# Four layer norms computed with a Newton root on VectorE instead of ScalarE's tables

## The reference, cut to what matters

```python
def _layernorm(x, axis=-1, eps=1e-05):
    m = jnp.mean(x, axis=axis, keepdims=True)
    v = jnp.var(x, axis=axis, keepdims=True)
    return (x - m) / jnp.sqrt(v + eps)
...
x = x + 0.5 * _L0_ffn_ref(_layernorm(x, axis=-1), ...)
x = x + _L0_attn_ref(_layernorm(x, axis=-1), ...)
x = x + 0.5 * _L0_ffn_ref(_layernorm(x, axis=-1), ...)
x = x + 0.5 * _L1_ffn_ref(_layernorm(x, axis=-1), ...)
x = x + _L1_attn_ref(_layernorm(x, axis=-1), ...)
x = x + 0.5 * _L1_ffn_ref(_layernorm(x, axis=-1), ...)
```

## Time and profile before

| | us |
|---|---|
| median of 3 runs | 1140.63 |
| lowest and highest | 1140.47, 1144.98 |
| the profiled execution, its own time | 1144.14 |
| span of its trace | 1142.4 |
| TensorE matmuls busy | 954.2 (84%) |
| VectorE busy | 672.9 (59%) |
| ScalarE busy | 626.3 (55%) |
| GpSimd busy | 349.1 (31%) |
| mean granted clock of TensorE | 0.894 of full |

### The profile page before, as it was taken

How to read it: one execution, slowest core, us unless ns; L and a number is a source line. 1 busy time by engine, 2 the same in 40 slices (tenths; PEclk the granted TensorE clock), 3 DMA queues, 4 the chain that set the end, 5 groups by cost and what they waited for, 6 DMA issues and landing times.

```text
span 1142.4 us, 12658 instructions
## 1 busy us (share of the span) xinstructions
PE 954.2 (84%) x4387; PEld 637.8 (56%) x4395; DVE 672.9 (59%) x1247; ACT 626.3 (55%) x986; POOL 349.1 (31%) x257
## 2 busy tenths in 40 slices
PE   6899997599999998689999974998567777675998
PEld 4678884233333333257888852886344554443797
DVE  2888885567777877437888826242645545226222
ACT  5455554378888887645555554445342544443443
POOL 1597775000000000006777725201011121204300
PEclk8999998789999999969999987999768877775999
DMA  5225110000000000033122101100000000001001
GB/s 162 40 83 155 58 66 8 0 1 1 1 1 0 1 1 1 0 97 73 64 64 65 47 1 55 38 1 1 1 2 3 3 3 2 2 1 37 1 1 37
DMA packets 30932, 33.61 MB, mean 29 GB/s; under 512 B 2254, under 2 KB 19990, under 8 KB 30870
## 3 DMA queue, kind: packets, MB, share of 16 engines
q1 hardware_dynamic: 30870, 32.82, 10.0%
HBM read 31.36 MB, written 1.18 MB: 28 GB/s over the span
## 4 chain that ended last, share of the span: by engine, by line
PE 63%; DVE 20%; ACT 10%; POOL 3%; issue 3%; DMA 0%; SPq 0%; ACTq 0%; DVEq 0%; POOLq 0%
PE ps L122 10%; PE ps L123 9%; PE ps L124 9%; PE ps L595 5%; PE ps L732 5%; DVE smax L1697 3%; PE ps L753 2%; PE ps L589 2%; PE ps L814 2%; PE ps L487 2%; PE ps L573 2%; ACT L1139 2%; ACT ex L1258 2%; PE ps L493 2%; PE ps L704 2%
## 5 line engine op out<-in xcount | busy, mean ns | idle before, releaser
L1800 POOL TENSOR_TENSOR fl<-fp,fh 128x512 fp32r<-128x512 f32 x144 | 225.6, 1588 | 128.5 <-ACT fh L1062 128.4
L1053 ACT ACTIVATE fs<-ps 128x512 f32<-128x512 f32 x144 | 86.2, 599 | 115.6 <-PE ps L124 115.3
L1396 DVE TENSOR_TENSOR fp<-fp,cwb 128x512 f32<-128x512 f32 x128 | 139.0, 1086 | 13.7 <-DVE fp L1389 0.5
L1389 DVE TENSOR_TENSOR fp<-fs,ps 128x512 f32<-128x512 f32 x144 | 98.1, 682 | 38.8 <-ACT fs L1053 37.6
L122 PE MATMUL ps<-z_hi,w_hi 128*128 128x512 f32 x288 | 116.7, 405 | 3.4 <-DVE fp L1389 3.3
L123 PE MATMUL ps<-z_lo,w_hi 128*128 128x512 f32 x288 | 115.7, 402 | 0.0
L124 PE MATMUL ps<-z_hi,w_lo 128*128 128x512 f32 x288 | 114.1, 396 | 0.0
L1062 ACT CAST fh<-fp 128x512 fp32r<-128x512 f32 x144 | 88.8, 617 | 34.7 <-DVE fp L1396 30.2
L1865 POOL TENSOR_TENSOR ln_sq<-ln_rs 128x512 f32<-128x512 f32 x20 | 21.1, 1056 | 272.8 <-ACT ln_rs L1102 272.8
L1858 POOL TENSOR_SCALAR_AFFINE_SELECT ex<-ex 128x1024 f32<-128x1024 f32 (+1 forms) x24 | 33.7, 1403 | 171.8 <-ACT ex L1258 171.8
L1697 DVE TENSOR_REDUCE smax<-ps 128x8 f32<-128x2048 f32 (+1 forms) x24 | 55.0, 2291 | 34.0 <-PE ps L828 27.3
(11 more groups left out here) (245 smaller groups left out, 2021.7 us busy)
## 6 DMA issues: line engine op xcount, KB each, us to landing
cwb<-cw_spread SPq DMA_DIRECT2D x64, 256.0 KB, 3.2
w_raw<-in_L_ffn_w_dram SPq DMA_DIRECT2D x20, 256.0 KB, 3.1
w_raw<-in_L_ffn_w_dram SPq DMA_DIRECT2D x4, 512.0 KB, 6.2
w<-in_L_ffn_w_dram SPq DMA_DIRECT2D x8, 256.0 KB, 5.4
x_tok<-in_L_attn_x_dram SPq DMA_DIRECT2D x4, 256.0 KB, 3.9
wb<-in_L_attn_W_dram SPq DMA_DIRECT2D x1, 1024.0 KB, 7.1
wb<-in_L_attn_W_dram SPq DMA_DIRECT2D x4, 256.0 KB, 4.1
stk<-mT SPq DMA_DIRECT2D x64, 4.0 KB
```

What stands on the lines that cost most here:

```text
L1053: act.activation(fs[:, n % 2, :], ps[:, n % 2, :], ACT.Silu).then_inc(silu_done, 1)
L1389: dve.tensor_tensor(f, fs[:, n % 2, :], ps[:, 2 + n % 2, :], ALU.mult).then_inc(prod_done, 1)
L1396: dve.tensor_tensor(f, f, cwb[:, x % CW_RING, :], ALU.mult).then_inc(weighed, 1)
L1800: pool.tensor_tensor(fl[:, n % RING0, :], fp[:, n % RING0, :], f32(fh[:, n % RING0, :]), ALU.subtract).then_inc(flo_done, 1)
```

## The change

The norms A to D take another path, and the table loads and the logarithms and exponentials of these four go. For a block `tb` of norm `n`:
- `ln_centre` on TensorE as before, but into banks of `LN_BANK`.
- `ln_square` on ScalarE, and `ln_copy`, which moves the centred block to `z`.
- `ln_variance` on TensorE: four matmuls with 128 tokens' squares as weights and one column of `mean_w`, so that the variance lies with tokens on partitions, one column for each 128 tokens.
- `ln_root` on VectorE: eleven small instructions, each of which waits for the one before, for blocks 0 to 2 together (12 columns) and then for block 3 (4 columns). A bit trick gives the first guess and three Newton steps follow.
- `ln_spread` on TensorE: four matmuls with one column of the root, repeated 128 times, as weights and the identity as the moving side, which lays the root out over the partitions again.
- `ln_scale` on VectorE multiplies; where halves are wanted, `ln_high` and `ln_low` follow.

The centring, squares and copies of blocks 0 to 2 are put into the end of the stage before, block 3 comes behind. The scores of `ffn1` go to bank 4 and move ahead of `ffn1` into the code of the norm.

```diff
-        XT1, SC1, PT1, GI1 = (4, 5, 6, 7), 0, 1, 2
...
+        XT1, SC1, PT1, GI1 = (5, 6, 7, 0), 4, 1, 2
...
+        LN_BANK = {LN_FFN0B: (4, 5, 6, 7), LN_FFN1: OUT0, LN_ATTN1: (0, 1, 6, 7), LN_FFN1B: (0, 1, 3, 5)}
+        LN_VAR = {LN_FFN0B: 3, LN_FFN1: 0, LN_ATTN1: 4, LN_FFN1B: 6}
...
+            def ln_centre(n, tb):
+                pe.wait_ge(ln_in, NTB * n + tb + 1)
+                pe.matmul(ps[:, LN_BANK[n][tb], :], centre[:], blk(xr, tb), start=True, stop=True).then_inc(lxc_ready, 1)
...
+            def ln_variance(n, tb):
+                pe.wait_ge(lsq_ready, later(n, tb))
+                for q in range(TPB):
+                    c = tb * TPB + q
+                    ins = pe.matmul(ps[:, LN_VAR[n], c:c + 1], LN_SQ[n][:, tb, q * P:(q + 1) * P], mean_w[:, 0:1], start=True, stop=True)
+                ins.then_inc(lvar_ready, 1)
+            def ln_spread(n, tb):
+                pe.wait_ge(root_ready, later(n, tb))
+                pe.wait_ge(lxc_copied, later(n, tb))
+                for q in range(TPB):
+                    ins = pe.matmul(ps[:, LN_BANK[n][tb], q * P:(q + 1) * P], ln_r[:, tb, q:q + 1].broadcast_to([P, P]), ident[:],
+                                    start=True, stop=True)
+                ins.then_inc(spread_ready, 1)
...
+            def scores(n, tb):
+                pe.wait_ge(z_ready, NTB * n + tb + 1)
...
-                logits(0)
-                up(0)
+                if call == 1:
+                    for tb in range(NTB - 1):
+                        ln_spread(ln, tb)
+                    ln_variance(ln, NTB - 1)
+                    pe.wait_ge(z_ready, u0 + 1)
+                    up(0)
+                    ln_spread(ln, NTB - 1)
+                    logits(0)
...
                 for n in range(ALL0 - LAG0, ALL0):
                     down(n)
+                    if call == 1 and n < ALL0 - 1:
+                        ln_centre(LN_FFN1, n - ALL0 + LAG0)
+                if call == 1:
+                    for tb in range(NTB - 1):
+                        ln_variance(LN_FFN1, tb)
+                    ln_centre(LN_FFN1, NTB - 1)
+                    for tb in range(NTB - 1):
+                        ln_spread(LN_FFN1, tb)
+                    ln_variance(LN_FFN1, NTB - 1)
+                    for tb in range(NTB - 1):
+                        scores(LN_FFN1, tb)
+                    ln_spread(LN_FFN1, NTB - 1)
+                    scores(LN_FFN1, NTB - 1)
...
+                for tb in range(NTB - 1):
+                    ln_centre(LN_FFN0B, tb)
+                for tb in range(NTB - 1):
+                    ln_variance(LN_FFN0B, tb)
...
+                ln_centre(LN_FFN0B, NTB - 1)
...
+                    if call == 0 and n == SEQS - 1:
+                        ln_centre(LN_ATTN1, 0)
+                        ln_centre(LN_ATTN1, 1)
...
+                if call == 0:
+                    ln_centre(LN_ATTN1, 2)
                 scatter(SEQS - 1)
...
-                layer_norm(u0, lambda tb: blk(xr, tb))
...
+                for tb in range(NTB - 1):
+                    ln_variance(LN_ATTN1, tb)
+                ln_centre(LN_ATTN1, NTB - 1)
+                for tb in range(NTB - 1):
+                    ln_spread(LN_ATTN1, tb)
+                ln_variance(LN_ATTN1, NTB - 1)
+                pe.wait_ge(y_done, NTB * HALVED.index(LN_ATTN1) + 2)
                 pe.wait_ge(z_ready, u0 + 1)
                 project_in(0, 0)
+                ln_spread(LN_ATTN1, NTB - 1)
                 pe.wait_ge(z_ready, u0 + NTB)
                 project_in(0, 1)
+                pe.wait_ge(cmask_done, 1)
...
+                    if s == SEQS:
+                        for t in range(NTB - 1):
+                            ln_centre(LN_FFN1B, t)
...
                 turn(NTB - 1)
+                for tb in range(NTB - 1):
+                    ln_variance(LN_FFN1B, tb)
                 project_out(NTB - 1)
+                for tb in range(NTB - 1):
+                    ln_spread(LN_FFN1B, tb)
+                ln_centre(LN_FFN1B, NTB - 1)
+                ln_variance(LN_FFN1B, NTB - 1)
+                for tb in range(NTB - 1):
+                    scores(LN_FFN1B, tb)
+                ln_spread(LN_FFN1B, NTB - 1)
+                scores(LN_FFN1B, NTB - 1)
...
+            def ln_square(n, tb):
+                act.wait_ge(lxc_ready, later(n, tb))
+                act.activation(LN_SQ[n][:, tb, :], ps[:, LN_BANK[n][tb], :], ACT.Square).then_inc(lsq_ready, 1)
+            def ln_copy(n, tb):
+                act.wait_ge(lxc_ready, later(n, tb))
+                act.copy(blk(z, tb), ps[:, LN_BANK[n][tb], :]).then_inc(lxc_copied, 1)
...
+                ln_square(LN_ATTN1, 3)
+                ln_copy(LN_ATTN1, 3)
+                ln_high(LN_ATTN1, 0)
+                ln_high(LN_ATTN1, 1)
+                ln_high(LN_ATTN1, 2)
+                act.preload_act_table_set(LN_EXP)
                 stack(0, 0)
+                ln_high(LN_ATTN1, 3)
                 stack(0, 1)
...
-            def layer_norm_whole(u0):
-                for tb in range(NTB):
-                    dve.wait_ge(rs_ready, u0 + tb + 1)
-                    dve.tensor_tensor(blk(z, tb), ps[:, BANK_XC + tb, :], ln_rs[:, tb, :], ALU.mult).then_inc(z_ready, 1)
...
+            def ln_root(n, first, last):
+                v, r, t = (x[:, first:last + 1, :] for x in (ln_v, ln_r, ln_t))
+                dve.wait_ge(lvar_ready, later(n, last))
+                own.did(dve.tensor_scalar(v, ps[:, LN_VAR[n], first * TPB:(last + 1) * TPB].rearrange("p (b q) -> p b q", q=TPB),
+                                          EPS_OUT, None, ALU.add))
+                own.wait()
+                own.did(dve.tensor_scalar(r.bitcast(I32), v.bitcast(I32), -0.5, ROOT_SEED, ALU.mult, ALU.add))
+                own.wait()
+                for step in range(ROOT_STEPS):
+                    own.did(dve.tensor_tensor(t, r, r, ALU.mult))
+                    own.wait()
+                    own.did(dve.scalar_tensor_tensor(out=t, in0=t, scalar=-0.5, in1=v, op0=ALU.mult, op1=ALU.mult))
+                    own.wait()
+                    ins = dve.scalar_tensor_tensor(out=r, in0=t, scalar=1.5, in1=r, op0=ALU.add, op1=ALU.mult)
+                    if step < ROOT_STEPS - 1:
+                        own.did(ins)
+                        own.wait()
+                ins.then_inc(root_ready, last + 1 - first)
+            def ln_scale(n, tb):
+                done = y_done if n in HALVED else z_ready
+                dve.wait_ge(spread_ready, later(n, tb))
+                dve.tensor_tensor(blk(z, tb), ps[:, LN_BANK[n][tb], :], blk(z, tb), ALU.mult).then_inc(done, 1)
...
+                    ln_root(ln, 0, 2)
+                    ln_scale(ln, 0)
+                    ln_scale(ln, 1)
+                    ln_low(ln, 0)
+                    ln_scale(ln, 2)
+                    ln_root(ln, 3, 3)
+                    ln_low(ln, 1)
+                    ln_low(ln, 2)
+                    ln_scale(ln, 3)
                 product(0)
+                if call == 1:
+                    ln_low(ln, 3)
...
+                if call == 1:
+                    ln_root(LN_FFN1, 0, 2)
+                    ln_root(LN_FFN1, 3, 3)
+                    for tb in range(NTB):
+                        ln_scale(LN_FFN1, tb)
...
                 stack(0, 0)
+                ln_scale(LN_ATTN1, 3)
+                ln_low(LN_ATTN1, 3)
                 stack(0, 1)
...
                 low(NTB - 1)
                 add(NTB - 1)
+                ln_root(LN_FFN1B, 0, 2)
+                ln_scale(LN_FFN1B, 0)
+                ln_root(LN_FFN1B, 3, 3)
+                ln_scale(LN_FFN1B, 1)
+                ln_scale(LN_FFN1B, 2)
+                ln_scale(LN_FFN1B, 3)
```

More of the change, by code:

```diff
@@ L509, in layer_norm @@
                 norm_parts(u0, src, busy)[1]()
+            def ln_centre(n, tb):
[16 more added lines that the diff above has]
+                pe.wait_ge(z_ready, NTB * n + tb + 1)
+                for t in range(tb * TPB, (tb + 1) * TPB):
+                    ins = pe.matmul(ps[:, SC1, t * EXP:(t + 1) * EXP], z[:, t * P:(t + 1) * P],
+                                    par[:, COL_GW:COL_GW + EXP], start=True, stop=True)
+                if tb == NTB - 1:
+                    ins.then_inc(sc_ready, 1)
             def ffn0(call, ln):
@@ L1047, in ffn0 @@
                 act.preload_act_table_set("silu_and_others")
+                if call == 1:
+                    ln_square(ln, NTB - 1)
+                    ln_copy(ln, NTB - 1)
+                    for tb in range(NTB - 1):
+                        ln_high(ln, tb)
                 def gate(n):
@@ L1078, in ffn0 @@
                     gate(n)
+                    if call == 1 and n == 0:
+                        ln_high(ln, NTB - 1)
                     if n == 1:
@@ L1167, in attn0 @@
                         fed(*rd)
+                for tb in range(NTB - 1):
+                    ln_square(LN_FFN0B, tb)
+                for tb in range(NTB - 1):
```

(14 more changed lines are left out.)

65 lines of the change are left out of this document (43 added, 22 removed).

## The result

The changed kernel took a median of 1160.12 us (four runs, 1157.88 to 1168.04) against 1142.81 for the kernel before (four runs): ratio 1.0164, interval 1.0106 to 1.0222, so 17 us slower. The forecast of 1150 had the right sign, but the time lies above its range, which ended at 1158.

A forecast was written before the change was run, and what follows sets the result against it. The prediction took the chain of waits (63% of the span on TensorE, 20% on VectorE) as the bound, with all four norms exposed. Norms A to D, -5 + 5 + 4.5 + 5 = +9.5, gave 1153.6, or 1150 for a median; range 1138 to 1158.

The forecast's parts named there:

- Prices: All norms: four small matmuls 0.9 us at full clock, 1.7 at half; centring 0.9, root 2.3, square 0.6, scaling 0.7.
- The bound for the spread: Spread of 128 columns, in no row: bounded by the same 0.9 us a group at full clock, 1.7 at half.
- A, -5 within -3 to -10.5: Norm A, priced by the start of `up(1)` against 509.83: -3 to -10.5 us, taken as -5.
- The bound of -10.5: Norm A at full clock: last root to 495.9 and four logit groups give 499.3 against 509.83.
- B, +5 within -0.3 to +7: Norm B, priced by the start of the transposes: 680.4 or 687.7 against 680.73, taken as +5 us.
- C, +4.5 within +3.5 to +7: Norm C, to the first attention product: +3.5 to +7 us against 811.08, memsets worth 0 to 2; +4.5 in all.
- D, +5 within 0 to +10: Norm D, priced by the start of the transposes: 1030.9 or 1040.6 against 1030.77, taken as +5 us.
- The sum, +9.5: Norms A to D: -5 + 5 + 4.5 + 5 = +9.5 us, which on the profiled 1144.14 gives 1153.6.
- "Minus 3.5" for the median: Whole kernel: the profiled execution stood 3.5 us above the median of 1140.63, so 1153.6 became a forecast of 1150.
- the third: Rival, norms: clock lost nearly throughout, or GpSimd holds up the roots; +14 to +21 us, 1155 to 1162; chance 0.12.
- The clock stays full: Rival, norms: spreads and centrings hold TensorE's full clock through the new gaps; about -7 us, 1133 to 1136; chance 0.13.
- The load's hidden cost: Rival, ScalarE: a table load holds it as long again; four fewer take another 5.1 us off, 1145; chance 0.02.

The follow-up runs named there:

- wide_var: The changed kernel with each variance matmul 128 columns wide instead of 1: median 1153.67 us, ratio 1.0083 to the kernel before.
- fill: The kernel with 128-column variances plus two unused 128x512 products in TensorE's waits in norms B and D: one execution, 1151.79 us against 1149.43 without them.
- tables: The kernel before with one more table load in each of its last four norms: one execution, 1146.87 us against a median of 1145.04 beside it.

## Why the prediction was right and wrong

- **Prices.** Right. A group of four took 0.9 to 1.0 at the full clock (12 thin matmuls in 2.73, 12 spreads in 2.94) and 1.7 at half, and a step of the root 0.20 to 0.21. The bound for the spread, which no row of before showed, held.
- **A, -5 within -3 to -10.5.** Measured -7.1: right, and sized too small. The 12 spreads ran at half clock (5.44), but the last four, behind a root, at the full one (1.16). (The bound of -10.5 left out that last spread: 495.9 and 0.9 for it and 3.6 for the logits give 500.4, so -9.4.)
- **B, +5 within -0.3 to +7.** Measured +6.5 against before's own execution, 5.4 against the others. The steps went as worked out: clock half at the scores, finished blocks waiting for the second root.
- **C, +4.5 within +3.5 to +7.** Measured +7.2, and +7.1 to the first attention product, as the forecast counted: just outside. The mechanisms are the ones named (scaling 3 and its halves behind the first stacking, memset on the root), but my value added only part of the half clock. The edits that took them out gave 1.1 for the memset, within the 0 to 2 allowed for it, and 3.8 for the order.
- **D, +5 within 0 to +10.** Measured +5.7. `project_out(3)` came 2.5 later, as summed at the full clock, and the spreads took 4.54, between the two bounds.
- **The sum, +9.5.** The four stretches give +12.2, which by itself is inside my range. **The step that failed is the one that was not there**: the sum had no term for anything outside the four norms, and the diff has one, three tiles of 64 bytes. They moved the weights and rings of the feed-forward stages and slowed TensorE there by 1.3%: 1.2 to 2.2 us in each of two stages, 4 to 6 us by the ratios. I had read the line that allocates them and asked only what uses them.
- **"Minus 3.5" for the median.** Weak: later medians of before were 1144.67 to 1147.77, so its profiled execution was an ordinary one and the three runs shown were low. From 1144, the forecast's own +9.5 and the missing 4 give 1158, and the norms' 12.2 in place of 9.5 gives 1160.
- **The rivals.** None held as a whole. The measured 1160 lies where the third put it, 1155 to 1162, but not for its reason: its norms would have cost +14 to +21, and they cost +12. It was right that GpSimd holds a root, in C alone. "The clock stays full" failed in B and D, where the spreads would have had to run at 0.9 a group; but `wide_var` and `fill` show that it was one edit away. The load's hidden cost is refuted by `tables`.

## What to carry to other kernels

A new small tile is a change to every tile allocated behind it: time a stage that the change does not touch, and put new tiles where nothing moves, or compare with an unused tile of the same size. A chain of thin matmuls and waits costs more than its instructions, through the clock behind it; a matmul of 128 columns costs hardly more than one of 1, and the clock stayed full behind it here. What one engine does for finished blocks belongs ahead of the next block's serial chain, where the other engine would wait for it. And a stage can get longer because the clock fell ahead of the edit: read where in the stretch the time went before blaming the edit.

## What was unexpected of the hardware

- 192 bytes more ahead of the tiles: matmuls of 512 columns 0.2321 to 0.2324 us apart instead of 0.2289 to 0.2292; 256 bytes more: 0.2290 to 0.2291.
- Two products that compute nothing, in a wait of TensorE, took 12 score matmuls from 5.01 to 2.85 us and norm B from 28.3 to 25.4.
- An integer operation on 12 elements a partition took 1.28 us beside a memset of GpSimd and 0.17 without it, while the nine operations behind it, with two inputs in SBUF each, took 0.17 each, also beside the next memset.
